# Attention and expert layer on one core: value products turned and turned back by VectorE in 32x32 blocks, the attention's low part by GpSimd

## The reference, cut to what matters

```python
x = x + xattn(layernorm(x), ctx)      # x, ctx: 128 sequences x 128 tokens x 256
x = x + ffn(layernorm(x))

# xattn: 16 heads of 16 dimensions
wq, wk, wv = q @ wq_w.T + wq_b, k @ wk_w.T + wk_b, v @ wv_w.T + wv_b    # q = layernorm(x), k = v = ctx
scores = einsum('bthd,bshd->bhts', wq, wk) / sqrt(16)
attn = einsum('bhts,bshd->bthd', softmax(scores, axis=-1), wv).reshape(b, t, d)
return attn @ wo_w.T + wo_b

# ffn: each token goes to the one of 8 experts with the highest logit; hidden size 64, exact GELU
```

## Time and profile before

| | us |
|---|---|
| median of 3 runs (range) | 1593.97 (1592.43 to 1604.42) |
| the profiled execution, whole | 1596.52 |
| its span in the profile | 1594.5 |
| PE busy in the span | 1506.3 (94%) |
| DVE busy | 1188.9 (75%) |
| ACT busy | 891.7 (56%) |
| POOL busy | 424.2 (27%) |

### The profile page before, as it was taken

One profiled execution on the slowest core, in us unless ns is written; L12 is line 12 of the kernel. 1 busy time (PEld: TensorE's weight loads), 2 busy tenths in 40 slices (PEclk: granted clock), 3 DMA queues, 4 the chain that ended last, 5 costly groups with the idle time before them and its releaser, 6 DMA issues.

```text
span 1594.5 us, 39584 instructions
## 1 busy us (share of the span) xinstructions
PE 1506.3 (94%) x15438; PEld 1210.1 (76%) x15438; DVE 1188.9 (75%) x2880; ACT 891.7 (56%) x1450; POOL 424.2 (27%) x600
## 2 busy tenths in 40 slices
PE   6899999999999999999999999879999999999998
PEld 5677777777778777878877787757777777777776
DVE  4787788767887788778777877667777777777775
ACT  4567666666667667767776777543342423333332
POOL 3223222222223223222322232112323232222221
PEclk9999999999999999999999999999999999999999
DMA  7466545554566556645654665402221212121221
GB/s 185 120 174 164 156 126 154 150 152 135 141 161 160 153 137 162 170 135 154 162 155 133 157 167 145 117 30 70 66 68 54 80 54 80 54 80 54 70 64 40
DMA packets 150480, 190.89 MB, mean 120 GB/s; under 512 B 17631, under 2 KB 101146, under 8 KB 150298
## 3 DMA queue, kind: packets, MB, share of 16 engines
q1 hardware_dynamic: 150298, 188.38, 43.1%
HBM read 53.01 MB, written 33.55 MB: 54 GB/s over the span
## 4 chain that ended last, share of the span: by engine, by line
PE 89%; DVE 5%; issue 3%; ACT 2%; DMA 1%; SPq 0%; ACTq 0%
PE s_ps L1195 12%; PE st_ps L1213 12%; PE pp_ps L1075 11%; PE pv_ps L1023 9%; PE s_ps L980 8%; PE pp_ps L1048 7%; PE st_ps L1008 7%; PE pp_ps L1083 5%; PE pp_ps L1069 4%; PE pv_ps L1031 3%; PE t_ps L999 3%; DVE negmax L729 2%; PE pp_ps L1161 2%; PE s_ps L1202 2%; ACT pT L636 1%
## 5 line engine op out<-in xcount | busy, mean ns | idle before, releaser
L729 DVE TENSOR_REDUCE negmax<-s_ps 128x8 f32<-128x1024 f32 x256 | 312.4, 1221 | 90.7 <-PE s_ps L980 83.4
L585 ACT ACTIVATE pT<-st_ps 128x1024 f32<-128x1024 f32 x256 | 262.7, 1026 | 101.9 <-PE st_ps L1008 101.8
L1213 PE MATMUL st_ps<-w_hi,q_packed 128*128 128x256 f32 x1024 | 213.2, 294 | 0.7 <-DVE q_packed L840 0.7
L1195 PE MATMUL s_ps<-k_packed,w_hi 128*128 128x512 f32 x512 | 172.8, 419 | 18.4 <-ACT pT L636 18.4
L1023 PE MATMUL pv_ps<-pT,v 128*32 128x128 f32 x4096 | 166.5, 278 | 24.8 <-DVE attn L742 12.5
L456 POOL TENSOR_TENSOR q_parts<-q,q_parts 128x1024 bf16<-128x1024 f32 x32 | 68.3, 2134 | 446.0 <-ACT q_parts L579 446.0
L980 PE MATMUL s_ps<-k_packed,q_packed 96*128 96x128 bf16 x2048 | 158.7, 221 | 18.4 <-issue 13.7
L1213 PEld LDWEIGHTS st_ps<-w_hi,q_packed 128*128 128x128 f32 x1024 | 168.4, 189 | 9.8 <-issue 6.4
L628 ACT ACTIVATE offhotT<-pv_ps 96x512 bf16<-96x512 bf16 x31 | 18.4, 592 | 253.1 <-PE pv_ps L1182 253.1
L1008 PE MATMUL st_ps<-q_packed,k_packed 98*128 98x128 bf16 x2048 | 158.9, 221 | 0.2 <-DMA q_packed<-negmaxT 0.2
L980 PEld LDWEIGHTS s_ps<-k_packed,q_packed 96*128 96x128 bf16 x2048 | 124.1, 98 | 44.3 <-issue 29.0
(11 more groups left out here) (179 smaller groups left out, 3511.7 us busy)
## 6 DMA issues: line engine op xcount, KB each, us to landing
q_packed<-q_parts SPq DMA_DIRECT2D x192, 256.0 KB, 3.8
k_packed<-k_parts SPq DMA_DIRECT2D x192, 256.0 KB, 4.4
xin<-in_x_dram SPq DMA_DIRECT2D x32, 512.0 KB, 3.8
cin<-in_ctx_dram SPq DMA_DIRECT2D x32, 512.0 KB, 3.9
x_scratch<-xb SPq DMA_DIRECT2D x32, 512.0 KB, 4.3
xin<-x_scratch SPq DMA_DIRECT2D x32, 512.0 KB, 4.6
out_dram<-xb SPq DMA_DIRECT2D x32, 512.0 KB, 3.2
q_packed<-negmaxT SPq DMA_DIRECT2D x128, 8.0 KB
```

What stands on the lines that cost most here:

```text
L585: a.activation(pT[u % 2][:], st_ps[:], ACT.Exp, scale=DH ** -0.5).then_inc(s_exp, 1)
L729: v.tensor_reduce(own, s_ps[:].rearrange("p (h s) -> p h s", s=P), AX_X, ALU.max, negate=True).then_inc(s_red, 1)
L1195: t.matmul(h_ps[m % 2], w[:, c, e, :].bitcast(F32R), x[n % 2][:, c, :].bitcast(F32R), start=(k == 0 and c == 0), stop=False)
L1213: t.matmul(o, h[n % 2][:, m, tok].bitcast(F32R), w[:, m, :].bitcast(F32R), start=(m == 0 and k == 0), stop=False)
```

## The change

For each batch VectorE turns `pv_ps` (128x512, f32) into `pv_by_q` in SBUF as 16 x 4 separate blocks of 32x32. Within the blocks queries and head rows change places; a partition then holds four queries of each block column, for one of four strips of heads. `norm` works on this layout, with the halves of the heads apart, and a second turn in blocks (128x256, SBUF to SBUF) brings the result back to the layout in which `project_out` wants it, except that its rows come in another order. That order is made good once, at the start: Wo's columns (four GpSimd copies into `wo_dense`) and the bias of v (two DMAs with strides in place of one) are laid out to match.

So TensorE's `turn_pv` and `turn_attn` are gone, ScalarE's `keep_pvT` too, and `keep_attn` reads SBUF. `values` of the next batch waits for the first turn, which stands ahead of the maxima of its unit, not for the norm. The low part of the attention is made by GpSimd, at units 0, 2, 4 and 6, ahead of what GpSimd has there; its residual moves from behind the second `lo` to unit 4. TensorE's `turn_max` no longer waits for the low part.

```diff
@@ start @@
+            pool.wait_ge(s_w[3], 16)
+            for co in range(C):
+                for c in range(C):
+                    g.tensor_copy(wo_dense[:, co, c * P:(c + 1) * P].rearrange("p (s f d) -> p s f d", s=STRIPS, f=2),
+                                  dense(w_in[3][:, co, :])[:, c]).then_inc(s_wd, 1)
@@ gpsimd @@
+            def rest_of_attn(n, b):
+                pool.wait_ge(s_ath, at(GB, n, b + 1))
+                hi, lo = aT[b % 2]
+                g.tensor_tensor(lo[:].bitcast(F32R), attnT[:], hi[:], ALU.subtract).then_inc(s_ate, 1)
             def group(n):
-                if n < LAST:
-                    lo(n + 1, 0)
-                if n + 2 <= LAST:
-                    norm(n + 2)
-                if n < LAST:
-                    lo(n + 1, 1)
-                    residual(n + 1)
+                for u in range(0, UNITS, 2):
+                    if turned_at(n, u):
+                        rest_of_attn(*turned_at(n, u))
+                    if u == 0 and n < LAST:
+                        lo(n + 1, 0)
+                    if u == 2 and n + 2 <= LAST:
+                        norm(n + 2)
+                    if u == 2 and n < LAST:
+                        lo(n + 1, 1)
+                    if u == 4 and n < LAST:
+                        residual(n + 1)
@@ scalar @@
-            def keep_pvT(n, b):
-                act.wait_ge(s_pv, at(UNITS, n, C * (b + 1)))
-                wait(act, s_tpv, at(GB, n, b))
-                a.copy(uvT[:], pv_ps[:]).then_inc(s_uv, 1)
@@ vector @@
+            def turn_values(n, b):
+                dve.wait_ge(s_pv, at(UNITS, n, C * (b + 1)))
+                wait(dve, s_nrm, at(GB, n, b))
+                v.transpose(pv_by_q[:], pv_ps[:]).then_inc(s_tpv, 1)
             def norm(n, b):
-                v.tensor_tensor(attn[:], pv[:, :, 0:DH], recip[:].unsqueeze(2).broadcast_to([P, H, DH]),
+                v.tensor_tensor(attn_by_half, pv[:, :, 0:DH].rearrange("p (f l) d -> p f l d", f=2),
+                                recip[:].rearrange("p (f l) -> p f l", f=2).unsqueeze(3).broadcast_to([P, 2, C * Q32, DH]),
                                 ALU.mult).then_inc(s_nrm, 1)
-            def rest_of_attn(n, b):
-                dve.wait_ge(s_ath, at(GB, n, b + 1))
-                hi, lo = aT[b % 2]
-                v.tensor_tensor(lo[:].bitcast(F32R), attnT_ps.rearrange("p (c t) -> p c t", c=C), hi[:],
-                                ALU.subtract).then_inc(s_ate, 1)
+                dve.wait_ge(s_nrm, at(GB, n, b + 1))
+                v.transpose(attnT[:].rearrange("p c t -> p (c t)"), attn[:]).then_inc(s_at, 1)
@@ vector, group @@
                     if more2 and u == 6:
-                        rest_of_attn(*done)
                         lower(n + 2, 3)
-                    if more2 and u == 5:
-                        norm(*done)
+                    if done and u % 2 == 1:
+                        turn_values(*done)
                     if later(n, u, 3):
                         maxima(*later(n, u, 3))
-                    if done and u % 2 == 1 and not (more2 and u == 5):
+                    if done and u % 2 == 1:
                         norm(*done)
@@ tensor @@
-            def turn_attn(n, b, kept):
-            def turn_pv(n, b):
                 if m == 0:
-                    wait(pe, s_nrm, at(GB, n, b))
+                    wait(pe, s_tpv, at(GB, n, b))
```

More of the change, by code:

```diff
@@ L158, in xattn_moe, with dense @@
         pp_ps = [psum(f"pp_ps{n}", [P, 512]) for n in range(2)]
-        pv = pv_ps[:].rearrange("p (h d) -> p h d", h=H)
-        attnT_ps = t_ps[:, 0:D]
+        Q32 = T // HP
+        STRIPS = P // HP
+        pv = pv_by_q[:].rearrange("p (l d) -> p l d", d=HP)
+        attn_by_half = attn[:].rearrange("p (l f d) -> p f l d", f=2, d=DH)
+        def dense(rows_of_w):
+            return rows_of_w.rearrange("p (f c s d) -> p c s f d", f=2, c=C, s=STRIPS)
         maxT_ps = t_ps[0:2 * H, D:D + P // 2].bitcast(BF16)
@@ L352, in _ @@
             load_weight(1)
-            for n, v in enumerate((bq, bk, bv)):
+            for n, v in enumerate((bq, bk)):
                 sp.dma_start(rows[n * C:(n + 1) * C, :], v.rearrange("(c p) -> c p", p=P)).then_inc(s_rows, 16)
+            for c in range(C):
+                row = 2 * C + c
+                sp.dma_start(rows[row:row + 1, :].rearrange("r (s f d) -> r s f d", s=STRIPS, f=2),
+                             dense(bv.rearrange("(a d) -> a d", a=1))[:, c]).then_inc(s_rows, 16)
             sp.dma_start(rows[3 * C:3 * C + MC, :], b1.rearrange("(m e) h -> m (e h)", e=EC)).then_inc(s_rows, 16)
@@ L513, in lo_of_xT, with group @@
                                 ALU.subtract).then_inc(f_xl, 1)
-            ffn_norm(0)
-            ffn_norm(1)
+            def group(n):
+                for u in range(0, UNITS, 2):
[9 more added lines that the diff above has]
+                        residual(n + 1)
+                    if u == 2 and n == LAST:
+                        ffn_norm(0)
+                    if u == 4 and n == LAST:
+                        ffn_norm(1)
+            for n in range(GROUPS):
+                group(n)
             lo_of_xT(0)
+            rest_of_attn(LAST, GB - 2)
+            rest_of_attn(LAST, GB - 1)
             def ffn_group(n):
@@ L574, in keep_attn @@
                 wait(act, s_y, at(GB, n, b - 1))
-                a.copy(aT[b % 2][0][:].bitcast(F32R), attnT_ps.rearrange("p (c t) -> p c t", c=C)).then_inc(s_ath, 1)
+                a.copy(aT[b % 2][0][:].bitcast(F32R), attnT[:]).then_inc(s_ath, 1)
             def mid(n, z):
@@ L593, in _ @@
             keep_weight(1)
-            act.wait_ge(s_rows, 16 * 4)
+            act.wait_ge(s_rows, 16 * 5)
             a.copy(rows_h[:].rearrange("r (d h) -> r d h", h=HC),
@@ L911, in group @@
                         stats_of(*rows_due)
-                    if done and u % 2 == 0 and not (more2 and u == 6):
-                        rest_of_attn(*done)
                     for rows_due in due:
@@ L938, in _ @@
                 group(n)
-            rest_of_attn(LAST, GB - 2)
+            turn_values(LAST, GB - 1)
+            norm(LAST, GB - 1)
+            route(0)
             residual(LAST, GB - 2)
-            route(0)
-            norm(LAST, GB - 1)
-            rest_of_attn(LAST, GB - 1)
             residual(LAST, GB - 1)
@@ L1025, in values @@
                 mm.then_inc(s_pv, 1)
-            def turn_pv(n, b):
-                pe.wait_ge(s_uv, at(GB, n, b + 1))
-                for k in range(4):
-                    mm = t.transpose(pv_ps[:, k * P:(k + 1) * P], uvT[:, k * P:(k + 1) * P], ident[:])
-                mm.then_inc(s_tpv, 1)
             def project_out(n, b):
@@ L1094, in turn_weight @@
             def turn_weight(k):
-                pe.wait_ge(s_w[k], 16)
+                if k < 3:
+                    pe.wait_ge(s_w[k], 16)
+                else:
+                    pe.wait_ge(s_wd, C * C)
                 for ci in range(C):
@@ L1104, in _ @@
                 turn_weight(k)
[L1105 removed]
+            pe.wait_ge(s_rows, 16 * 5)
             t.transpose(pv_ps[:, 0:NR], rows[:], ident[0:NR, 0:NR])
@@ L1236, in odd @@
             def odd(n, u):
-                ahead, nxt, done = later(n, u, 3), later(n, u, 1), turned_at(n, u)
+                ahead = later(n, u, 3)
                 if ahead:
```

36 lines of the change are left out of this document (9 added, 27 removed).

## The result

| | us |
|---|---|
| kernel before, median of 4 runs (range) | 1593.3 (1592.4 to 1604.4) |
| changed kernel, median of 4 runs (range) | 1637.3 (1634.9 to 1644.0) |
| ratio, 95% interval | 1.027 (1.021 to 1.032) |
| forecast | 1645.0, range 1570 to 1670, slower 0.67 |

The change makes the kernel 44 us slower, by an amount that the forecast has 8 us too high. TensorE lost 64 us of busy time, VectorE gained 149.

The account below looks back on a forecast made before the run. Despite TensorE's 89% of the chain, each group was taken as three stretches, also bound by VectorE and a DMA. Groups +51, start +3.5, end -4 gave +50 on 1596.5: 1647, or 1645 us against the runs' median; range 1570 to 1670.

Parts of the forecast that it names:

- VectorE's lag: At the start of a group's unit 0, VectorE's first remainder comes some 1.4 us behind TensorE, from 0.03 ahead.
- The collision: In unit 0 the third maxima operation starts 0.2 us inside GpSimd's lo and stands until its end: 2.0 us a group.
- Stretch B: From unit 0's first remainder on VectorE to unit 2's turned maxima: falls from 11.3 to 10.2 us, VectorE ending last.
- The turns: VectorE's added block turns: 0.60 us for 128x512 out of PSUM, 0.34 for the 128x256 turn back.
- Rival 3: VectorE's block turns run at half rate: 2.2 us a group more, +66 us, 1711; chance 0.08.
- The small collisions: VectorE's maxima operations meet GpSimd's small operations in unit 2 and its residual in unit 5: 0.2 us each a group.
- The loop: One group of eight units: -0.7 + 2.0 + 0.2 + 0.2 = +1.7 us, +51 us over 30 groups.
- The stretches: A group's three parts, cut at unit 0's first remainder, unit 2's turned maxima, unit 5's scores: 12.4, 10.2, 8.3 us uncollided.
- the gain without the collision: A group takes 30.9 us against 31.6: 0.7 us less, 21 us over 30 groups.
- The start: GpSimd's first norm stands behind four copies waiting for Wo, 4.2 us late: counted +3.5 us, bounds 2 and 5.
- GpSimd's low parts: The attention's low parts on GpSimd have over 0.5 us to spare: cost 0, or 0.7 us a batch without that.
- Rival 2: TensorE bounds after all and its 0.9 us a batch comes off, 119 us in all: 1479; chance 0.06.

Follow-up runs that it names:

- lo_after_maxima: Changed kernel with one more wait: GpSimd starts the first lo of a group only when unit 0's three maxima operations are done; 1575.9 us, 0.989 of before.
- third_one_source: Changed kernel with its third maxima operation as a copy of one SBUF tensor instead of a difference of two; 1576.3 us, 0.988 of before.
- before_no_turns: Kernel before without TensorE's six transpositions a batch, ScalarE's copy and the low part's wait for the turned maxima, nothing added on VectorE; 1551.5 us, 0.973.
- one_maximum_all: Changed kernel without the two small maxima operations, first norm ahead of Wo's copies, last k pack ahead of the store, residual behind unit 6's low part; 1504.1 us.
- filled_wait: Changed kernel with 16 identity transpositions on TensorE ahead of the turned maxima in unit 0, where it waits for VectorE; 1634.9 us, 1.023 of before.

## Why the prediction was right, point by point

- **VectorE's lag** into unit 0: 1.4 us forecast, 1.42 measured at both places looked at (the group shown, and the median of groups 1 to 29).
- **The collision**: forecast for the third maxima operation of unit 0, by a margin of 0.2 us, 2.0 us long. Measured 0.15 us and 1.99 us, in 28 groups. It was shown to be on the path by lo_after_maxima, and to need two SBUF operands by third_one_source and the additions of L763. This one step decides the sign: without it 1575.9 us. It was right with little to spare: in group 15 the second operation met lo instead.
- **Stretch B without it**: 10.2 forecast, 10.2 measured (lo_after_maxima). That VectorE ends last there fits lo_after_maxima, where it is busy 9.9 of the 10.2 us in the mean and TensorE 8.9, and the changed kernel, where it is busy 11.55 of 11.86 us in the group shown. My reason for B in the kernel before was short: VectorE's busy 9.37 us are there, but what ties TensorE to them is the wait of the values for the norm, which before_no_turns showed.

```profile
617.15:629.01 11.86, 8.93 (x100) 7.13 (x98) 11.55 (x25) 7.25 (x11) 5.07 (x7) 1.00 0.72 178
```

- **The turns**: 0.60 and 0.34 us a step forecast from a subtraction and a product. The lengths are 0.71 and 0.45, the steps to the next start 0.63 (622.66 to 623.29) and 0.37. Rival 3, half rate, had 1.2 and 0.7 and is out.
- **The small collisions** were forecast in units 2 and 5, 0.2 us each. In unit 2 there is none: the mean excess of 0.07 us is one operation of 2.14 us in group 5. In unit 5 it is 0.06 us. One of 0.56 us in unit 4, where the second operation starts within GpSimd's low part, was not forecast; TensorE waits for the landing there, so it should cost little, which no run tried alone.
- **The loop**: +1.7 us a group forecast, +1.4 measured (31.9 to 33.3). The group of 33.3 itself is right. Its base was not: 31.6 us came from one group and from a mean in which the short last group counts, while the middle groups took 31.9. That is 0.3 x 30 = 8 us, nearly all of the miss. The stretches are right to 0.1 us each (12.6, 12.4 and 8.3 forecast; 12.6, 12.5 and 8.2 measured), but that of B is in part luck. Its terms were 0.4 us too high: the small collision of unit 2 is not there, and 2.0 us is the whole length of the operation, of which 0.17 was in the 10.2 already. TensorE's clock, which the forecast did not have, adds 0.5 us to B (12.47 in all groups, 11.92 in those without a fall in it). Within the prediction the stretches of before sum to 31.8 us, and the new 30.9 was compared with 31.6, so the gain without the collision, given as 0.7, was 0.9 by its own terms.
- **The start**: +3.5 us forecast. The groups start at 51.2 us, not 47.6, and norm moved from 6.97 to 10.80. With the norm ahead again they start at 47.8 and 47.5 in two kernels, but at 50.6 in one_maximum_all, so the norm is not all of it. Its worth in the time stays within the spread of the runs.

```profile
9.84 0.98 POOL L458 COPY pv_by_q<-pT 128x128 f32<-128x128 f32 x4 [7.28 <-DMA pT<-in_L_xattn_wo_w_dram]
10.80 0.19 POOL L464 TENSOR_TENSOR ve<-mv,eps 128x4 f32<-128x4 f32 x1
```

- **GpSimd's low parts at cost 0, and 0.7 us a batch without them**: they hold TensorE up for 0.8 us in all in the changed kernel. On VectorE they cost 63 us in 128 batches, 0.49 a batch, as long as the collision is there.
- **Rival 2**, TensorE's 119 us come off: before_no_turns, where VectorE gets nothing added, gives 42.
- **Not forecast**: TensorE's clock, at half for 104 us, not 25. By the groups it costs B 0.8 us in 19 of 29, some 16 us; in filled_wait B gained 13 of them and the time hardly any.

## What to carry to other kernels

A small VectorE operation on two SBUF tensors is priced by the GpSimd operation that it may meet, not by its own 0.17 us; give such an operation one source, or have GpSimd start behind it. Before work is moved off the engine with 89% of the chain, look in each stretch for the wait that ends last: here VectorE and one DMA stood right behind it, and the relief paid 18 us with the collision away and 50 with room on VectorE. Each time a bound was moved, the two engines met at another place; so an order tuned for one bound, as that of the residual, has to be looked at again after the next.

## What the hardware showed beyond that

- A block turn of 128x512 f32 out of PSUM takes 709 ns on VectorE, and 445 ns for 128x256 from SBUF to SBUF; a subtraction and a product of these shapes take 680 and 420.
- The rule of two SBUF sources holds for 128x256 too: the product grows from 0.42 to 0.74 us behind GpSimd, while the addition of the same shape with one source in PSUM stays at 0.42 us inside lo.
- Idleness of 2.3 us in one unit of a group goes with TensorE's clock at half for 104 us of 1633, and with 0.8 us more in the stretches B that have such a time in them. Filling that wait with idle work, down to 0.6 us of idleness, leaves no B with such a time and 63 us in all.
